# The later layers of a plain row stream one turn back, and a mark table awaited by its first scan instead of by the stage that loads it

## The reference, cut to what matters

```
x = _layernorm(x + _L0_gnn_ref(...))   # 4 attention (GAT) layers, softmax per destination, layernorm
x = _layernorm(x + _L1_gnn_ref(...))   # 3 relation layers: relu(h[src] + relv[rel]), mean per destination
x = _layernorm(x + _L2_gnn_ref(...))   # 3 SAGE layers: h @ Ws.T + mean(h[src]) @ Wn.T + b
x = _layernorm(x + _L3_gnn_ref(...))   # tensor product over edges
```

```
h = x @ W;  alpha = leaky_relu((h @ a_s)[src] + (h @ a_d)[dst] + (ea @ We) @ a_e)
out = segment_sum(h[src] * softmax_per_dst(alpha)) + b;  out = layernorm(out) * g + beta
```

```
L1: h = cell(x);  h += cell(relu(ln(h)));  h += cell(relu(ln(h)));  out = ln(h)
L2: h = relu(x @ Ws0.T + n0 @ Wn0.T + b0); h = relu(h + h @ Ws1.T + n1 @ Wn1.T + b1)
    out = h @ Ws2.T + n2 @ Wn2.T + b2
```

## Time and profile before

| | |
|---|---|
| median of 3 runs | 5012.12 us (5004.49 to 5012.53) |
| profiled execution | 5035.27 us |
| its span, first to last instruction | 5033.5 us |
| mean granted TensorE clock | 0.858 |
| PE busy | 3759.1 us, 75% of the span |
| PEld busy | 3111.3 us, 62% |
| DVE busy | 3757.5 us, 75% |
| ACT busy | 3210.8 us, 64% |
| POOL busy | 2801.2 us, 56% |

### The profile page before, as it was taken

One profiled execution on the slowest core, in us unless ns is written; L12 is line 12 of the kernel. 1 busy time (PEld: TensorE's weight loads), 2 busy tenths in 40 slices (PEclk: granted clock), 3 DMA queues, 4 the chain that ended last, 5 costly groups with the idle time before them and its releaser, 6 DMA issues. The chain is left out here.

```text
span 5033.5 us, 104447 instructions
## 1 busy us (share of the span) xinstructions
PE 3759.1 (75%) x23663; PEld 3111.3 (62%) x23663; DVE 3757.5 (75%) x10843; ACT 3210.8 (64%) x11475; POOL 2801.2 (56%) x2759
## 2 busy tenths in 40 slices
PE   6355889966786677767776878878698997967775
PEld 5254778855556554745575555556587886856664
DVE  1576789978878886978696877879687786747665
ACT  2022779967887686868685543358698795646554
POOL 0473767711760375047302767767476776757776
PEclk9699999978998798979876767779899998978777
DMA  8899999955885597568665446657599896862221
GB/s 180 111 289 284 358 371 317 284 151 157 265 271 153 164 295 247 148 193 278 226 181 150 151 150 184 202 171 240 192 344 327 293 354 223 246 140 61 64 69 52
DMA packets 918273, 1074.23 MB, mean 213 GB/s; under 512 B 202779, under 2 KB 565065, under 8 KB 917106
## 3 DMA queue, kind: packets, MB, share of 16 engines
q1 hardware_dynamic: 763570, 890.24, 54.1%
q0 software_dynamic: 90944, 180.06, 14.1%
q10 hardware_dynamic: 63556, 1.81, 1.8%
HBM read 509.54 MB, written 566.14 MB: 214 GB/s over the span
## 5 line engine op out<-in xcount | busy, mean ns | idle before, releaser
L2366 POOL DMA_INDIRECT H<-gat_rows,src_i x784 | 801.1, 1022 | 876.0 <-POOLq L80 638.0
L1917 POOL DMA_INDIRECT s_G<-sage_rows,src_i x588 | 595.3, 1012 | 286.4 <-issue 175.9
L1696 POOL DMA_INDIRECT r_G<-rel_rows,idx x392 | 404.6, 1032 | 165.9 <-issue 116.7
L2555 PE MATMUL p_M<-Wg,p_hT 128*128 128x132 f32 x2352 | 342.3, 290 | 59.3 <-DVE p_res L2612 45.3
L2555 PEld LDWEIGHTS p_M<-Wg,p_hT 128*128 128x128 f32 x2352 | 296.8, 196 | 106.6 <-issue 91.4
L2612 DVE SCALAR_TENSOR_TENSOR p_res<-p_M,p_rr,cg 128x132 f32<-128x132 f32 x1176 | 333.8, 346 | 2.7 <-PE p_M L2555 1.7
L2694 PEld LDWEIGHTS p_pl_p<-Wn,p_pl_h 128*128 128x128 f32 x1568 | 204.1, 197 | 205.4 <-ACT p_pl_h L2788 158.5
L1305 PE MATMUL d_S<-ones,d_sqT 128*128 128x1 f32 x1568 | 227.6, 266 | 135.6 <-DVE d_ve L1450 135.6
L1709 PE MATMUL r_t<-r_oh,relv 8*128 8x512 f32 x294 | 203.9, 779 | 166.1 <-DMA r_G<-rel_rows,idx 79.0
L2694 PE MATMUL p_pl_p<-Wn,p_pl_h 128*128 128x128 f32 x1568 | 223.3, 287 | 136.2 <-ACT p_pl_h L2788 136.2
L1305 PEld LDWEIGHTS d_S<-ones,d_sqT 128*128 128x128 f32 x1568 | 221.9, 218 | 162.4 <-issue 128.9
(11 more groups left out here) (483 smaller groups left out, 12423.8 us busy)
## 6 DMA issues: line engine op xcount, KB each, us to landing
gat_rows<-p_res SPq DMA_DIRECT2D x294, 264.0 KB
sage_rows<-p_pl_s SPq DMA_DIRECT2D x294, 256.0 KB
gat_rows<-x_row SPq DMA_DIRECT2D x98, 536.0 KB
gat_rows<-d_res SPq DMA_DIRECT2D x147, 264.0 KB
d_hs<-gat_rows SPq DMA_DIRECT2D x147, 256.0 KB
s_hT<-sage_slots_t SPq DMA_DIRECT2D x147, 256.0 KB
slot_rows<-H SPq DMA_DIRECT2D x49, 544.0 KB, 11.4
x_x<-in_x SPq DMA_DIRECT2D x98, 256.0 KB
```

The source lines that it names most:

```text
L1696: pool.indirect_dma_start(self.G[:, g % 4, k, :], None, table, bass.IndirectOffsetOnAxis(index[:, c:c + 1], 0), bounds_check=bound, oob_is ...
L1917: pool.indirect_dma_start(self.G[:, g % 4, k, :], None, kn.st[self.l], bass.IndirectOffsetOnAxis(kn.idx[:, c:c + 1], 0), bounds_check=boun ...
L2366: pool.indirect_dma_start(kn.H[:, c, 0:width], None, table, bass.IndirectOffsetOnAxis(index[:, c:c + 1], 0), bounds_check=bound, oob_is_er ...
L2555: mm = pe.matmul(self.pM[self.bank(b, j)][:, k // 2, (k % 2) * TW:(k % 2 + 1) * TW], self.hT[l][:, b.s2, k * P:(k + 1) * P], kn.Wg[:, l, : ...
```

## The change

Two parts.

**Marks.** A new `Pass` (`marks0` to `marks3`, and `marks4` around `constants` and the three relation stages) owns the buffer of the mark table and a semaphore `same_in`. SP's transfer counts on this semaphore and SP no longer waits. DVE waits for it before the first scan of each `d` stage and before the first scan of `r0`. Each of the five new passes closes with a clearing of semaphores and a barrier of its own.

**Lags.** In `Plain` seven kinds of steps move back by one turn, the order of the lists stays: `last`, `rows2` (6 to 7), `rows1`, `hidden2` (5 to 6) on PE; `keep_rows(2)` (6 to 7), `keep_h2` and `keep_rows(1)` (5 to 6) on ACT; `keep_z` (6 to 7) on DVE; `store_rows(2)` (6 to 7), `store_rows(1)` (5 to 6) and `store_z` (7 to 8) on SP.

```diff
--- before.py
+++ after.py
@@ -424,13 +424,14 @@
                     else:
                         self.plain_rows(l, first, (self.NBLK - first) // (4 - l))
                         first += (self.NBLK - first) // (4 - l)
-                    with ExitStack() as marks:
-                        self.same = marks.enter_context(nc.sbuf_tensor(f"same_run{l}", [P, ND], U8))
+                    with Pass(nc, f"marks{l}") as marks:
+                        self.same, self.same_in = marks.sb("same_run", [P, ND], U8), marks.sem("same_run_in")
                         self.soft(l)
                         self.slots(l)
             self.same = keep("same_run", [P, ND], U8)
             self.shares = keep("share_squares", [P, K, P])
-            with ExitStack() as relation:
+            with ExitStack() as relation, Pass(nc, "marks4") as marks:
+                self.same_in = marks.sem("same_run_in")
                 self.constants(relation)
                 for l in range(3):
                     self.run(f"r{l}", lambda q: RelSlots(self, q, l))
@@ -1158,15 +1159,13 @@
             psa, psb, psc, psd = (q.ps(n) for n in ("a", "b", "c", "d"))
             pen = q.sb("pen", [HALF, 2, 2, P])
             pen_carry = q.sb("pen_carry", [HALF, 2, 2, P])
-            held = q.sem("marks_in")
             ch, pe_s, dn = q.sem("steps"), q.sem("turned"), q.sem("weights_shifted")
             block = q.block()
             flat = lambda ap: ap.rearrange("r g p -> r (g p)")
 
             @block.sync
             def _(sp):
-                sp.dma_start(self.same[:, :], self.same_d.partition_broadcast(P)).then_inc(held, 16)
-                sp.wait_ge(held, 16)
+                sp.dma_start(self.same[:, :], self.same_d.partition_broadcast(P)).then_inc(self.same_in, 16)
 
             @block.vector
             def _(v):
@@ -1441,6 +1440,8 @@
                     done(v, yr if end else wm, b, 4)
                     done(v, sq, b, 4)
                     first = isinstance(b.n, int) and b.n == 0
+                    if first:
+                        v.wait_ge(self.same_in, 16)
                     v.tensor_tensor_scan(yT[:, b.s4, :], self.same[:, bass.ds(b.n * BLOCK, BLOCK)], pT[b.s2][:, :],
                                          0.0 if first else yT[:, (b.m - 1) % 4, BLOCK - 1:BLOCK], ALU.mult, ALU.add).then_inc(scn, 1)
 
@@ -1787,6 +1786,8 @@
 
         def run_sums(b):
             done(v, self.mtk, b)
+            if self.l == 0 and isinstance(b.n, int) and b.n == 0:
+                v.wait_ge(kn.same_in, 16)
             done(v, self.scn, b, 1)
             done(v, self.wm, b, self.Y)
             run_scan(v, kn, b, self.agT[:, b.m % self.Y, :], self.agT[:, (b.m - 1) % self.Y, BLOCK - 1:BLOCK], self.pt[b.m % len(self.pt)][:, :]).then_inc(self.scn, 1)
@@ -2679,7 +2680,7 @@
             done(sp, self.on_z_kept, b)
             sp.dma_start(kn.z_at(b.n + self.lo), self.zT[:, b.s2, :]).then_inc(self.zst[b.s2], 16)
 
-        steps = [(load, -2), (load_x, -1), (store_rows(0), 5), (store_rows(2), 6), (store_rows(1), 5), (store_z, 7), (store_n0, 2)]
+        steps = [(load, -2), (load_x, -1), (store_rows(0), 5), (store_rows(2), 7), (store_rows(1), 6), (store_z, 8), (store_n0, 2)]
         return [(s, lag + 2, self.n) for s, lag in steps]
 
     def stores_landed(self, sp):
@@ -2731,7 +2732,7 @@
             done(pe, self.rows_kept[2], b, 1)
             rows_of(self.p2, self.h2[:, b.s2, :], kn.Wn[:, 2, :], self.rows_made[2])
 
-        return [(s, lag + 2, self.n) for s, lag in ((last, 6), (rows2, 6), (turn, 4), (rows1, 5), (hidden2, 5), (rows0, 4), (hidden1, 4))]
+        return [(s, lag + 2, self.n) for s, lag in ((last, 7), (rows2, 7), (turn, 4), (rows1, 6), (hidden2, 6), (rows0, 4), (hidden1, 4))]
 
     def scalar(self, act):
         kn, eps = self.kn, self.kn.eps_c[:, 0:1]
@@ -2793,8 +2794,8 @@
             done(act, self.on_made_z, b, 2)
             act.activation(self.h2[:, b.s2, :], self.ph2[:, :], ACT.Relu, bias=kn.sb[:, 1:2]).then_inc(self.on_kept_h2, 1)
 
-        steps = [(keep_h1, 5), (keep_rows(0, self.p0), 5), (keep_rows(2, self.p2), 6), (keep_n1, 4), (deviation_u, 3),
-                 (keep_h2, 5), (keep_rows(1, self.p1), 5), (square3, 0), (norm, 2), (deviation2, 1), (deviation3, 0), (square_u, 2)]
+        steps = [(keep_h1, 5), (keep_rows(0, self.p0), 5), (keep_rows(2, self.p2), 7), (keep_n1, 4), (deviation_u, 3),
+                 (keep_h2, 6), (keep_rows(1, self.p1), 6), (square3, 0), (norm, 2), (deviation2, 1), (deviation3, 0), (square_u, 2)]
         return [(s, lag + 2, self.n) for s, lag in steps]
 
     def vector(self, v):
@@ -2869,7 +2870,7 @@
             self.pair_landed(v, self.zst, b)
             v.scalar_tensor_tensor(self.zT[:, b.s2, :], self.pz[:, :], kn.sb[:, 2:3], self.nT[:, b.s4, :], ALU.add, ALU.add).then_inc(self.on_z_kept, 1)
 
-        steps = [(scale2, 2), (scale3, 1), (sums_u, 3), (keep_z, 6), (shift, 2), (gamma, 1), (scale_u, 3),
+        steps = [(scale2, 2), (scale3, 1), (sums_u, 3), (keep_z, 7), (shift, 2), (gamma, 1), (scale_u, 3),
                  (n1, 3), (add_x, 1), (stats, 1), (aggregate, 1), (sums3, 0), (add_shared, 2)]
         return [(s, lag + 2, self.n) for s, lag in steps]
```

## The result

| | before | after |
|---|---|---|
| median (runs) | 5004.49 us (5) | 4984.68 us (5) |
| range | 5000.35 to 5012.53 | 4982.53 to 4995.06 |
| profiled execution | 5035.27 us | 4991.18 us |

The ratio is 0.9964, with a 95% interval of 0.9949 to 0.9978: some 18 us faster (19.8 us between the medians). The three runs of before that stood ahead of the prediction had a median of 5012.12; with two more it is 5004.49.

A forecast was written before the change was run, and what follows sets the result against it. ACT with PE was taken to set a turn at 7.29 us, DVE's ring close behind at 7.24. Full turns -11.3, their end -2.8, head -6.0, tail +10.8, constants marks -2.0, passes +1.7 gave -9.6 us: 5002.5, range 4988 to 5014.

The forecast's parts named there:

- What bounds a turn: Undisturbed full turns: ACT with PE sets 7.29 us before; after the change the DVE ring sets 7.24 us.
- The term of the full turns: The 80 full turns of the `p` stages: 7.24 us each plus 25 us of z waits, -11.3 us.
- (c): Rival, chance 0.07: in the full turns keep_z waits for late z landings in most turns; kernel slower, 5025.5 us.
- The second stall: Full turns: after a late DVE, PE slows and ACT waits longer for hidden2; these 12.7 us go.
- No clock term: PE in full turns: few turns pay for slow products after a gap, so the sum holds nothing for the clock.
- that rule alone: PE's gaps: if waits between matmuls left following ones cold in every turn, closing all gaps would give back 44 us.
- Head: Start of each `p` stage: the slow turn at the first hidden2 gets shorter, -2.0 us a stage, -6.0 in all.
- Last two turns: End of the full turns, where ACT alone paces: its 0.46 us wait goes, -2.8 us in all.
- Tail: End of each `p` stage: one more turn of emptying on PE, 3.6 us a stage, +10.8 in all.
- Marks: Soft stages gain 0, the constants boundary -2.0 us, closing five new passes costs +1.7 us.
- (b): Rival, chance 0.21: z waits stay below 17 us, head and tail end well; -24 us, 4988.
- (a): Rival, chance 0.25: DMA engines set the pace, full turns gain nothing; 5013.8 us, no change.

The follow-up runs named there:

- e4: The changed kernel with a ring of four buffers for z instead of two; ratio 0.9948 of the kernel before.
- e3: The kernel before with a ring of four buffers for z instead of two, nothing else; ratio 0.9953 of the kernel before.
- e8: The changed kernel with the z store as the first transfer of a turn on SP; ratio 0.9950 of the kernel before.
- e12: The changed kernel measured once more, unaltered; ratio 0.9968 of the kernel before, median 4991.6 us.
- e2: The kernel before with the marks part of the change alone, lags as before; ratio 0.9995 of the kernel before.
- e6: The changed kernel with the z store moved behind n0's store in SP's list; ratio 1.0083 of the kernel before.
- e5: The kernel before with the z store moved ahead of rows1's store in SP's list; ratio 0.9966 of the kernel before.

## Why the prediction was wrong

The sum was -9.6 us; the ratio says -18. The forecast of 5002.5 stood besides on a median of three runs, 5012.12, that later runs put at 5004.5 to 5007. So 7.6 of the miss of 17.8 us are the base, and the sum gave some 8 to 10 us too little. It would have been further off without luck: the full turns came out 16.9 us better than forecast and the tails 6.4 us worse. By its steps:

- **What bounds a turn: right.** 7.21 us against 7.24, the DVE ring; the head turns without keep_z took 6.56 us, 0.65 less. The full turns gained no part of PE's 136 us.
- **The term of the full turns was the step that failed.** "I take z waits of 25 us instead of 17.1": they were 7.5. The rest of that term held, 80 x 7.24 + 7.5 = 586.7 against 587.3, though two small errors cancel in it: without z waits 80 turns took 577.9 us (e4), not 579.2, and a z wait costs 1.25 times its length, not once. Two reasons for it fell. "0.92 busy at 7.69 us a turn would be a full 1.0 at about 7.05 us" was an extrapolation; e3, with more buffers, and e8, with an earlier store, ran at 0.94 to 0.96 busy and 7.2 to 7.3 us a turn without one z wait. And rival (c) said "the store leaves no later against keep_z than before" and left it there: it leaves 0.6 us sooner, since the relu that stands ahead of rows1's copy on ACT no longer waits for hidden2. On a grace of 3.7 us against landings of 4.8 this decides. I had both rows and didn't follow SP's list through them. The second stall, 12.7 us of late turns, went as said, and it was a consequence of the first, as the prediction had it: e3 has neither.
- **No clock term: right.** Each turn of the changed kernel still has a gap on PE (1.26 us ahead of rows0 at 1395.44), and the eight products behind it still take 1.16 us, at a granted clock of 0.99 to 1.00 over the full turns. So the 44 us that "that rule alone" would give back were not to be had. The passage of the Trainium skill that the prediction cites for it (TensorE: Matmul & The Clock Gate, section Loop structure matters more than you think) speaks of a long wait for a DMA between matmuls, which no undisturbed turn here has.
- **Head: right in size.** -6.0 forecast, -6.8 in the first three turns, and 2.0 more in the fourth turns, inside the full ones. **Last two turns:** -2.8 forecast, -2.2.
- **Tail: mis-sized.** +10.8 forecast, +17.2 measured (+13.4 in e12). A round takes 4.55 us, not 3.66: I added hidden2 to the way from last to hidden2 and left out the relu between them, 1.81 - 1.02 = 0.8 us. An undisturbed tail grew by 4.2 to 4.3 us (`p3`, and `p2` in e12). Most of the rest is in `p1`, 8.3 us, past the 5 us that the prediction named as a sign of being wrong: there the late z landing took some 3 us. In e12, without such a landing, `p1`'s tail grew by 5.0 us and ends on POOL's gathers. So "POOL's gathers are unchanged and done before" holds for `p2` and `p3`, and for `p1` only while something else is later.
- **Marks: right.** Soft stages 0; constants -1.8 (forecast -2.0); a pass 0.43 to 0.45 us where it can be read, behind the `d` stages (forecast 0.33 each). The forecast net was -0.3 us; e2 can't be told from no change. The Trainium skill (DMA: Bandwidth & Descriptors, Rules for kernel authors) advises to issue early and wait late; the trace agrees at the one place where nothing hid the wait, with 1.8 us, and shows nothing at the four where arithmetic did.
- **Rivals.** The result came out beside (b), the ring runs clean, which had 0.21; its terms were full turns -22 (measured -28), tail +8 (+17), head -7 (-7). (a), that the DMA engines set the pace, is refuted by e3. (c) is what e6 made: with 54.7 us of z waits its sum would give full turns of 579.2 + 54.7 = 633.9 us; e6 took 638.4 and was slower than before. (By its own terms (c) loses 10 us from (10 - 1.7 + 36.3) / 80 = 0.56 us a turn, not 0.58.)

## What to carry to other kernels

Of a ring with a store behind it, work out the grace: when the store leaves on its queue, when the buffer is wanted again, and how that compares with the longest landings in the trace. If a transfer that frees a buffer stands in its queue behind one that waits for another engine, move it ahead first: one step moved in SP's list (e5, 0.9966) gave as much here as turning a pipeline back by a turn (0.9964 to 0.9968). And read a tail by its whole round, with each step that another engine puts between two of one engine, and look at which stream ends the stage once the first one is quicker.

## What the runs showed of the hardware that was not expected

- The landing of one 256 KB store took from 2.4 us in a tail of before (2469.24 to 2471.65, a DMA share of 0.56 in that stretch) over 3.9 to 5.8 us in the full turns of before (mean share 0.90 to 0.92) to 5.5 us in the tail of the changed kernel's `p1` (1472.38 to 1477.91, a share of only 0.60). The mean hides much: over the landing of 4.77 us at 1303.80 the share was 1.03 and 350 GB/s were moved (packets are counted where they start, so it can pass 1). A mean share of 0.92 was no bound: 0.96 and 298 GB/s were reached in e8 without a z wait.
- A z wait of DVE cost 1.8 to 2.0 times its own length as long as PE and ACT handed h1 and h2 to each other within a turn, and 1.1 to 1.3 times once they handed them over from one turn to the next.
- The granted clock of the full turns followed the waits: 0.93 in e6 with 54.7 us of z waits, 0.97 to 0.98 before, 1.00 in e3 without any. Within a late turn of before it was 1.00 ahead of an idle stretch of 2.38 us on PE and 0.57 to 0.63 in the 4.2 us behind it; behind the usual idle stretch of 1.34 us the products ran at full pace (1.16 us).
- One more pass, with nothing in it but a clearing of semaphores and a barrier of all engines, takes 0.43 to 0.45 us.
